# Layer 2 of a four-layer kernel: when VectorE adds an expert's output, and when two router and step-size pieces are issued

## The chip, the core and the metric

The kernel runs on one core of one Trainium2 chip. The metric is the device time of one execution in microseconds (us). The engines are TensorE (PE in the rows; PEld is its weight load), VectorE (DVE), ScalarE (ACT), GpSimd (POOL) and SyncE (SP). Each works through its own instructions in order and waits for the others at semaphores.

## The reference, cut to layer 2

Four layers, each `x = x + s * silu(f)` on 4 sequences of 512 tokens with 128 features, where `s` is a sequence mixer of the normed input and `f` a mixture of experts of the same input. The change is in layer 2: a selective scan, and 8 experts of which two count for a token.

```
dbc = einsum('ble,fe->blf', x_main, W_x)
dt_raw, Bm, Cm = dbc[..., :64], dbc[..., 64:80], dbc[..., 80:]
dt = softplus(einsum('blr,er->ble', dt_raw, W_dt) + b_dt)      # 256 step sizes a token
def step(h, inp):                                              # 16 states a feature
    h = exp(dt_t[..., None] * A) * h + dt_t[..., None] * B_t[:, None, :] * x_t[..., None]
    y = einsum('ben,bn->be', h, C_t)
...
logits = silu(xt @ rw1 + rb1) @ rw2 + rb2
w = softmax(where(mask_of_top_2, logits, -inf), axis=1)        # the shares
h = silu(einsum('nd,edh->enh', xt, we1) + be1)                 # 8 experts, 512 hidden
eo = einsum('enh,ehd->end', h, we2) + be2
y = xt + einsum('ne,end->nd', w, eo)
```

## The kernel before, in words

The four sequences are the batches b = 0 to 3 (`B`), a sequence is 4 tiles of 128 tokens (`T`), and layer 2 goes through 16 state steps a batch (`NS`), 64 in all: step k is step n = k % 16 of batch k // 16. The order on every engine is written out by hand in one loop over k for each; nothing schedules it.

In step k VectorE does, in this order: scan(k), the recurrence over all 512 tokens for both halves of the 256 features (one 128x1024 instruction, L2430 in the rows, with both its operands in SBUF); outs(k-1), two products with C (L2438, one operand in PSUM); inputs(k+2), the product of dt\*x with B (L2423, one operand in PSUM). After them, in even steps, comes add_expert: four additions of 128x128 (L2454), one for each tile of tokens, each of which adds one expert's output, weighed by its share, to `ACC2`. Steps 2, 4, 6, 7, 10, 11 and 13 hold more: normalisation, the second half of the last batch's output (L2483 first), the choice of experts, `split`, `share` (L2387 first; it needs the exponentials that ScalarE makes in share_exp) and dt_sums (L2408, L2410, then L2415 in dt_x). Step 12 holds `correction` (L2401) between the scan and outs.

GpSimd adds every product of outs to `YY` (L1985, two instructions a step, all operands in SBUF). H has four buffers.

TensorE in its step k: chunk(2k), the second product of an expert, c_row(k), which spreads C for outs(k) into a PSUM bank and waits for outs(k-1) to have read it, chunk(2k+1), b_row(k+3), the same for inputs(k+3), then one of the jobs that share PSUM bank 0 ("spare" jobs, table `front_order`), two hidden products of an expert, and then any second spare job of the step. In step 9 the spare jobs are the two products for the step sizes of the next batch, ("dt", 0) ahead of the hidden products and ("dt", 1) behind them. A spare job waits until its forerunner's bank has been read.

ScalarE makes the decays (L2270, two steps' worth in each even step, `wide` in the rows), the silus of the hidden products (L2258, four in each odd step), and for the next batch dt_parts (L2217, L2218), dt_exp (L2222), share_exp (L2226) and others.

Of the kernel before, what the change touches and what calls it, by code (L numbers as in the profile page):

```python
# [27 lines left out]
T = S // P  # L28
# [5 lines left out]
def build(nc, I, out):  # L34
    ctx = ExitStack()
    with ctx:
# [378 lines left out]
        def lsem(name):  # L415
            h = scope[0].enter_context(nc.semaphore(name))
            lsems.append(h)
            return h
# [1449 lines left out]
        def layer2(fcT, pjT, feats, wide, XM, mv3, rstd3):  # L1868
# [10 lines left out]
            hp, hs, op_, ad = (lsem(f"f2_{k}") for k in ("hidden", "silus", "chunks", "added"))  # L1879
# [9 lines left out]
            def use(*key):  # L1889
                uses[key] = len(uses)  # L1890
            front_order = {4: (("xnt",),), 5: (("r1",),), 6: (("logits",),), 7: (("c", 0), ("c", 1)), 8: (("dbc",),),
                           9: (("dt", 0), ("dt", 1)), 14: (("wT",),)}
            for key in (("xnt",), ("c", 0), ("c", 1), ("r1",), ("dbc",), ("dt", 0), ("dt", 1), ("logits",), ("wT",)):
                use(key[0], 0, *key[1:])
            first_bank = {("r1",): 5, ("c", 0): 6, ("c", 1): 7, ("dt", 0): 6, ("dt", 1): 7}
# [6 lines left out]
            for k in range(NK):  # L1902
                b, n = divmod(k, NS)
# [16 lines left out]
            def read(*key):  # L1920
                return uses[key] + 1

            with ExitStack() as c:
# [26 lines left out]
                with nc.Block() as block:  # L1950
# [216 lines left out]
                    def _(act):  # L2167
# [124 lines left out]
                        for k in range(NK):  # L2292
                            b, n = divmod(k, NS)
                            more = b + 1 < B
                            if n % 2 == 0 and k + 2 < NK:
                                decays(k + 2)
                                decays(k + 3)
                            if n == 7 and more:
                                x_silu(b + 1, 0)
                            if n == 9 and more:  # L2300
                                dt_parts(b + 1, 0)
                            if n == 13:
                                z_silu(b, 0)
                            if n == 1 and b:
                                gate(b - 1)
                            if n % 2 and k + 1 < NK:
                                for i in range(4):
                                    hidden(2 * k + 2 + i)
                            if n == 3 and more:
                                apply_in(b + 1)  # L2310
                            if n == 5 and b:
                                apply_out(b - 1)
                            if n == 4 and more:
                                turn_in(b + 1)
                            if n == 5 and more:
                                router(b + 1)
                            if n == 7 and more:
                                x_silu(b + 1, 1)
                            if n == 8 and more:
                                dbc(b + 1)  # L2320
                                d_term(b + 1)
                            if n == 9 and more:
                                dt_parts(b + 1, 1)
                            if n == 10 and more:
                                dt_exp(b + 1)
                                share_exp(b + 1)
                            if n == 12 and more:
                                dt_log(b + 1)
                            if n == 13:
                                z_silu(b, 1)  # L2330
                            if n == 14 and more:
                                store_wT(b + 1)
                            if not more and n in (3, 6, 9):
                                early_apply(n // 3 - 1)
                            if not more and n in (4, 7, 14):
                                early_turn((4, 7, 14).index(n))
# [15 lines left out]
                    def _(v):  # L2352
# [90 lines left out]
                            nc.vector.tensor_tensor(ACC[:, :, :].rearrange(flat), o, XN4[:, b, :, :].rearrange(flat),  # L2443
                                                    ALU.add).then_inc(m0, 1)

                        def add_expert(j):
                            b, e = divmod(j, NE)
                            v.wait_ge(op_, 4 * j + 4)
                            if e:
                                v.wait_ge(ad, j)  # L2450
                            else:
                                v.wait_ge(m0, read("bias", b))
                            for t in range(T):
                                last = nc.vector.scalar_tensor_tensor(ACC[:, t, :], PS[:, 6 + j % 2, t * P:(t + 1) * P],  # L2454
                                                                      WG2[:, b % 2, t, e:e + 1], ACC[:, t, :], ALU.mult, ALU.add)
                            last.then_inc(ad, 1)

                        def gated(b):
                            v.wait_ge(m0, read("z", b, 1))
# [44 lines left out]
                        for k in range(NK):  # L2504
                            b, n = divmod(k, NS)
                            more = b + 1 < B
                            scan(k)
                            if k == 0:
                                share(0)
                            if n == 12 and more:  # L2510
                                correction(b + 1)
                            if n == 1 and b:
                                gated(b - 1)
                            if n == 2:
                                biases(b)
                            if n == 4 and b:
                                take_out(b - 1)
                            if n == 7 and more:
                                take_logits(b + 1)
                            if k:  # L2520
                                outs(k - 1)
                            if k + 2 < NK:
                                inputs(k + 2)
                            if n % 2 == 0 and k:
                                add_expert(k // 2 - 1)
                            if n == 2 and more:
                                stats_in(b + 1)
                            if n == 4 and b:
                                out_stats(b - 1)
                            if n == 6 and b:  # L2530
                                finish(b - 1)
                            if n == 7 and more:
                                choose(b + 1)
                            if n == 10 and more:
                                split(b + 1)
                            if n == 11 and more:
                                share(b + 1)
                            if n == 13 and more:
                                dt_sums(b + 1)
                                dt_x(b + 1)  # L2540
                            if not more and n in (2, 5, 8):
                                early_stats((2, 5, 8).index(n))
# [12 lines left out]
                        for t in range(T):  # L2555
# [3 lines left out]
                            last = nc.vector.tensor_tensor(X4[:, B - 1, t, :], x, rest[:, t, :], ALU.add)  # L2559
# [710 lines left out]
```

## Time and profile before

| | us |
|---|---|
| median of 3 runs (lowest to highest) | 1391.28 (1389.5 to 1394.29) |
| the profiled execution: time | 1392.78 |
| the profiled execution: span from first to last instruction | 1391.0 |
| mean granted TensorE clock | 0.922 of full |
| layer 2's state steps | about 758 to 1178 in the span |

The profile is one execution. Its time is 1.5 us above the median, and 1.8 us lie outside its span. Busy shares are given for each engine; a wait is idle time of an engine just before an instruction, put down to the engine that ended it.

### The profile page before, as it was taken

The numbers are of one execution on the slowest core, as the hardware profiler recorded it, in microseconds if no ns is written. First come the engines' busy times: TensorE is split into PE (matmuls) and PEld (weight loads), VectorE is DVE, ScalarE is ACT, GpSimd is POOL, SyncE is SP. The second block draws the span as 40 slices with busy tenths as digits, with TensorE's granted clock in tenths as the row PEclk, the third lists the DMA queues.
The fourth block names the chain that finished last, engine by engine and source line by source line (L and its number), as shares of the span: only waits on it lengthen the run. The fifth ranks groups of instructions, "written<-read, shape, count | busy, mean of one in ns | idle before, by whom it ended". The sixth has DMA issues, their size and how long they took to land. (4 is left out here: it accounts for less than half of the span.)

```text
span 1391.0 us, 21029 instructions
## 1 busy us (share of the span) xinstructions
PE 1151.0 (83%) x7010; PEld 811.3 (58%) x7010; DVE 999.5 (72%) x2280; ACT 763.7 (55%) x1586; POOL 614.8 (44%) x607
## 2 busy tenths in 40 slices
PE   3999999999898879367766888888888977889995
PEld 1455665665465568156653655655645655668885
DVE  2466767678787727277765989989998999535555
ACT  1456556555544527144446867667768675345552
POOL 4243445444336834554100533733643565216672
PEclk9999999999999989589987999999899889799997
DMA  7400000000000023550000000000000000101113
GB/s 176 121 1 1 1 1 1 1 1 1 1 5 22 28 63 116 154 163 16 1 13 0 1 1 1 1 1 1 1 1 1 1 1 0 31 10 40 43 44 107
DMA packets 54443, 40.71 MB, mean 29 GB/s; under 512 B 13185, under 2 KB 46687, under 8 KB 54337
## 3 DMA queue, kind: packets, MB, share of 16 engines
q1 hardware_dynamic: 40994, 27.58, 6.8%
q0 software_dynamic: 4544, 9.32, 2.4%
q10 hardware_dynamic: 8800, 2.48, 0.9%
q8 instruction: 58, 0.95, 0.3%
q14 instruction: 47, 0.39, 0.1%
HBM read 26.32 MB, written 13.04 MB: 28 GB/s over the span
## 5 line engine op out<-in xcount | busy, mean ns | idle before, releaser
L780 POOL TENSOR_TENSOR PR<-PR,R 128x512 f32<-128x512 f32 (+3 forms) x128 | 160.3, 1264 | 233.1 <-DVE R L1275 232.5
L1985 POOL TENSOR_TENSOR YY<-YY,H 128x512 f32<-128x512 f32 x120 | 164.1, 1390 | 182.0 <-DVE H L2438 182.0
L410 PE MATMUL banks<-XT,we 128*128 128x128 f32 (+1 forms) x568 | 175.8, 442 | 14.0 <-ACT HH L2258 13.7
L1074 ACT ACTIVATE PR<-banks,NM 128x257 f32<-128x257 f32 (+3 forms) x256 | 132.2, 526 | 94.7 <-DVE NM L1247 93.0
L410 PEld LDWEIGHTS banks<-we,HH 128*128 128x128 f32 x1024 | 144.9, 205 | 35.7 <-issue 31.2
L2430 DVE TENSOR_TENSOR_SCAN H<-wide,H 128x1024 f32<-128x1024 f32 x64 | 164.1, 2564 | 0.2
L410 PE MATMUL banks<-we,HH 128*128 128x128 f32 x1024 | 145.1, 288 | 0.0
L410 PEld LDWEIGHTS banks<-XT,we 128*128 128x128 f32 x568 | 89.5, 201 | 65.5 <-issue 41.2
L2258 ACT ACTIVATE HH<-banks,be1f 128x512 f32<-128x512 f32 x128 | 83.4, 685 | 73.7 <-PE banks L410 72.8
L410 PE MATMUL banks<-BCR,SEL 96*128 96x512 f32 x128 | 67.1, 526 | 63.8 <-DVE H L2438 55.4
L410 PEld LDWEIGHTS banks<-PTS,V 128*64 128x64 f32 x1152 | 65.7, 138 | 83.4 <-issue 48.5
L410 PE MATMUL banks<-PTS,V 128*64 128x128 f32 (+1 forms) x1152 | 93.1, 296 | 24.1 <-issue 11.0
L1247 DVE TENSOR_REDUCE NM<-banks 128x2 f32<-128x514 f32 (+3 forms) x128 | 102.7, 823 | 3.3
L1256 DVE COPY PTS<-banks 128x384 f32<-128x384 f32 (+1 forms) x96 | 57.5, 599 | 60.7 <-PE banks L936 59.8
L410 PE MATMUL banks<-KT,QT 64*128 64x384 f32 (+3 forms) x512 | 96.2, 474 | 1.5 <-issue 0.8
L936 PE MATMUL banks<-ident,PR 128*128 128x128 f32 x640 | 92.5, 285 | 2.1 <-POOL PR L780 1.8
L936 PEld LDWEIGHTS banks<-ident,PR 128*128 128x128 f32 x640 | 73.4, 145 | 31.6 <-issue 31.6
L2438 DVE TENSOR_TENSOR H<-H,banks 128x512 f32<-128x512 f32 x128 | 80.8, 671 | 7.5 <-PE banks L410 7.5
L2270 ACT ACTIVATE wide<-feats,Aneg 128x512 f32<-128x512 f32 (+1 forms) x128 | 81.9, 710 | 0.4
L2423 DVE TENSOR_TENSOR H<-DTX,banks 128x1024 f32<-128x1024 f32 x64 | 77.5, 1212 | 1.1 <-PE banks L410 0.9
L410 PEld LDWEIGHTS banks<-BCR,SEL 96*128 96x128 f32 x128 | 26.3, 206 | 72.0 <-DVE H L2438 61.9
L2747 POOL DMA_INDIRECT XS<-xrows,GIX x39 | 38.3, 982 | 53.5 <-DVE GIX L3157 37.3
(568 smaller groups left out, 2445.9 us busy)
## 6 DMA issues: line engine op xcount, KB each, us to landing
xsort<-zrow SPq DMA_DIRECT2D x1, 3072.0 KB, 13.6
XS<-xsort SPq DMA_DIRECT2D x12, 256.0 KB, 2.9
ysort<-PTS SPq DMA_DIRECT2D x12, 256.0 KB, 2.2
pj_stage<-in_L_ffn_w_proj SPq DMA_DIRECT2D x1, 2048.0 KB, 11.9
we<-in_L_ffn_we SPq DMA_DIRECT2D x1, 2048.0 KB, 15.3
we<-yrows SPq DMA_DIRECT2D x8, 256.0 KB, 5.4
xrows<-XN SPq DMA_DIRECT2D x4, 256.0 KB, 3.4
out<-XN SPq DMA_DIRECT2D x4, 256.0 KB, 2.3
```

The source lines that it names most:

```text
L410: return nc.tensor.matmul(o, l, r, start=start, stop=stop)
L780: last = nc.gpsimd.tensor_tensor(p, p, R[:, T * q + t, :].unsqueeze(2).to_broadcast([P, 2, w]), ALU.mult)
L936: last = nc.tensor.transpose(PS[:, 4 + s, k * P:(k + 1) * P], PR0[:, q % 2, s, a:a + P], ident[:, :])
L1074: nc.scalar.activation(PR0[:, q % 2, s, OFF[t]:OFF[t] + w], ps2(n)[:, s, SLOT[t]:SLOT[t] + w], ACT.Exp, bias=NM[:, m, s:s + 1], accum_out= ...
L1247: last = nc.vector.tensor_reduce(NM[:, T * q + t, :], ps2(n)[:, :, SLOT[t]:SLOT[t] + (t + 1) * P + more], AX.X, ALU.max, negate=True)
L1256: nc.vector.tensor_copy(PTS[:, m % 2, 1, 0:w], PS[:, 5, 0:w]).then_inc(ptB, 1)
L1985: nc.gpsimd.tensor_tensor(YY[:, m, :], YY[:, m, :] if n else XD[m], H[:, k % 4, m, :], ALU.add).then_inc(ya, 1)
L2258: nc.scalar.activation(HH[:, i, :], PS[:, 3 + g % 3, :], ACT.Silu, bias=be1f[:, j % NE, i:i + 1]).then_inc(hs, 1)
L2270: nc.scalar.activation(DA[:, k % 4, m, m:], DT[:, b % 2, m, m:], ACT.Exp, scale=Aneg[:, m, n:n + 1]).then_inc(ex, 1)
L2423: nc.vector.tensor_tensor(H[:, k % 4, :, :], DTX[:, b % 2, :, :], PS[:, 1, :].unsqueeze(1).to_broadcast([P, 2, S]), ALU.mult).then_inc(bm, 1)
L2430: nc.vector.tensor_tensor_scan(h, DA[:, k % 4, :, :].rearrange("p m s -> p (m s)"), h, 0.0, ALU.mult, ALU.add).then_inc(scn, 1)
L2438: nc.vector.tensor_tensor(h, h, PS[:, 2, :], ALU.mult).then_inc(hc, 1)
```

## The change

Three things move; nothing is removed or added to the computation. In step 0 VectorE still adds the last batch's eighth expert whole. For the other experts it adds tiles 0 and 1 in an even step and tiles 2 and 3 in the odd step behind it, and tells TensorE that the bank is free only after the second half. `share` moves from step 11 to step 12. The product ("dt", 1) moves from the end of TensorE's step 9 to the place of step 10's first spare job, and ScalarE's dt_parts for it from step 9 to step 10, ahead of dt_exp.

```diff
--- before.py
+++ after.py
@@ -1889,7 +1889,7 @@
             def use(*key):
                 uses[key] = len(uses)
             front_order = {4: (("xnt",),), 5: (("r1",),), 6: (("logits",),), 7: (("c", 0), ("c", 1)), 8: (("dbc",),),
-                           9: (("dt", 0), ("dt", 1)), 14: (("wT",),)}
+                           9: (("dt", 0),), 10: (("dt", 1),), 14: (("wT",),)}
             for key in (("xnt",), ("c", 0), ("c", 1), ("r1",), ("dbc",), ("dt", 0), ("dt", 1), ("logits",), ("wT",)):
                 use(key[0], 0, *key[1:])
             first_bank = {("r1",): 5, ("c", 0): 6, ("c", 1): 7, ("dt", 0): 6, ("dt", 1): 7}
@@ -2319,9 +2319,8 @@
                             if n == 8 and more:
                                 dbc(b + 1)
                                 d_term(b + 1)
-                            if n == 9 and more:
+                            if n == 10 and more:
                                 dt_parts(b + 1, 1)
-                            if n == 10 and more:
                                 dt_exp(b + 1)
                                 share_exp(b + 1)
                             if n == 12 and more:
@@ -2443,17 +2442,18 @@
                             nc.vector.tensor_tensor(ACC[:, :, :].rearrange(flat), o, XN4[:, b, :, :].rearrange(flat),
                                                     ALU.add).then_inc(m0, 1)
 
-                        def add_expert(j):
+                        def add_expert(j, tiles=range(T)):
                             b, e = divmod(j, NE)
                             v.wait_ge(op_, 4 * j + 4)
                             if e:
                                 v.wait_ge(ad, j)
                             else:
                                 v.wait_ge(m0, read("bias", b))
-                            for t in range(T):
+                            for t in tiles:
                                 last = nc.vector.scalar_tensor_tensor(ACC[:, t, :], PS[:, 6 + j % 2, t * P:(t + 1) * P],
                                                                       WG2[:, b % 2, t, e:e + 1], ACC[:, t, :], ALU.mult, ALU.add)
-                            last.then_inc(ad, 1)
+                            if tiles[-1] == T - 1:
+                                last.then_inc(ad, 1)
 
                         def gated(b):
                             v.wait_ge(m0, read("z", b, 1))
@@ -2521,8 +2521,10 @@
                                 outs(k - 1)
                             if k + 2 < NK:
                                 inputs(k + 2)
-                            if n % 2 == 0 and k:
+                            if n == 0 and k:
                                 add_expert(k // 2 - 1)
+                            elif n > 1:
+                                add_expert(k // 2 - 1, (0, 1) if n % 2 == 0 else (2, 3))
                             if n == 2 and more:
                                 stats_in(b + 1)
                             if n == 4 and b:
@@ -2533,7 +2535,7 @@
                                 choose(b + 1)
                             if n == 10 and more:
                                 split(b + 1)
-                            if n == 11 and more:
+                            if n == 12 and more:
                                 share(b + 1)
                             if n == 13 and more:
                                 dt_sums(b + 1)
```

VectorE, batch 0's steps 11 and 12 before: `wide` holds the decays, `PR` and `OH` lead to the shares (`WG`), `EW` is the exponential of dt. Line numbers of the kernel before.

```order
L2430 SCALAR_TENSOR_TENSOR H<-wide,H 128x1024
L2438 TENSOR_TENSOR H<-H,banks 128x512 x2
L2423 TENSOR_TENSOR H<-DTX,banks 128x1024
L2387 TENSOR_TENSOR PR<-PR,OH 128x4x8
L2388 TENSOR_REDUCE rt<-PR 128x4
L2389 RECIPROCAL rt<-rt 128x4
L2390 TENSOR_TENSOR WG_9025<-PR,rt 128x32
L2430 SCALAR_TENSOR_TENSOR H<-wide,H 128x1024
```

The same steps in the changed kernel, where lines from here on have numbers lower by one: first step 11, then step 12 up to the scan of step 13.

```order
L2429 SCALAR_TENSOR_TENSOR H<-wide,H 128x1024
L2437 TENSOR_TENSOR H<-H,banks 128x512 x2
L2422 TENSOR_TENSOR H<-DTX,banks 128x1024
L2453 SCALAR_TENSOR_TENSOR ACC_9023<-banks,WG_9025,ACC_9023 128x128 x2
L2429 SCALAR_TENSOR_TENSOR H<-wide,H 128x1024
```

```order
L2429 SCALAR_TENSOR_TENSOR H<-wide,H 128x1024
L2400 TENSOR_SCALAR DTX<-EW 128x1024
L2401 TENSOR_TENSOR DTX<-EW,DTX 128x1024
L2437 TENSOR_TENSOR H<-H,banks 128x512 x2
L2422 TENSOR_TENSOR H<-DTX,banks 128x1024
L2453 SCALAR_TENSOR_TENSOR ACC_9023<-banks,WG_9025,ACC_9023 128x128 x2
L2386 TENSOR_TENSOR PR<-PR,OH 128x4x8
L2387 TENSOR_REDUCE rt<-PR 128x4
L2388 RECIPROCAL rt<-rt 128x4
L2389 TENSOR_TENSOR WG_9025<-PR,rt 128x32
```

Step 11 has two additions and no share rows; step 12 has two additions, and the four share rows stand behind them.

ScalarE, steps 9 to 10 of batches 0 to 2, as a difference: `feats` and `EW` are written by dt_parts, `wide` by the decays.

```order
+L2270 ACT_TABLE_LOAD
+L2270 ACTIVATE wide<-feats,Aneg 128x512
+L2270 ACTIVATE wide<-feats,Aneg 128x511
+L2270 ACTIVATE wide<-feats,Aneg 128x512
+L2270 ACTIVATE wide<-feats,Aneg 128x511
 L2217 ACTIVATE feats<-banks,bdt 128x512
 L2218 ACTIVATE EW<-banks,bdt 128x512
-L2270 ACT_TABLE_LOAD
-L2270 ACTIVATE wide<-feats,Aneg 128x512
-L2270 ACTIVATE wide<-feats,Aneg 128x511
-L2270 ACTIVATE wide<-feats,Aneg 128x512
-L2270 ACTIVATE wide<-feats,Aneg 128x511
```

The four decays come ahead of the second dt_parts instead of behind it; dt_exp and share_exp follow both.

TensorE, from the product ("dt", 0) of its step 9 on: `XNT,WdtT` are the dt products, `XT,we` hidden products, `we,HH` chunks, and `BCR,SEL` c_row, then b_row.

```order
 L410 MATMUL banks<-XNT,WdtT 128x512
 L410 MATMUL banks<-XT_9022,we_7451 128x512 x2
+L410 MATMUL banks<-we_7452,HH 128x128 x4
+L410 MATMUL banks<-BCR,SEL 128x512
+L410 MATMUL banks<-we_7452,HH 128x128 x4
+L410 MATMUL banks<-BCR,SEL 128x512
 L410 MATMUL banks<-XNT,WdtT 128x512
-L410 MATMUL banks<-we_7452,HH 128x128 x4
-L410 MATMUL banks<-BCR,SEL 128x512
-L410 MATMUL banks<-we_7452,HH 128x128 x4
-L410 MATMUL banks<-BCR,SEL 128x512
 L410 MATMUL banks<-XT_9022,we_7451 128x512 x2
```

Both chunks, c_row(10) and b_row(13) now come ahead of ("dt", 1).

## Rows read from the trace of the kernel before

**Rows 1.** The page, part 1: busy time, share of the span, instructions.

```profile
PE 1151.0 (83%) x7010; PEld 811.3 (58%) x7010; DVE 999.5 (72%) x2280; ACT 763.7 (55%) x1586; POOL 614.8 (44%) x607
```

**Rows 2.** Busy us by engine in layer 2; then TensorE clock and DMA.

```profile
740.00:1180.00 440.00, 359.41 (x1659) 244.17 (x1658) 410.99 (x599) 311.69 (x435) 206.04 (x164) 0.91 0.00 1
```

**Rows 3.** Group of the scans there: busy us, mean ns, idle before.

```profile
L2430 DVE TENSOR_TENSOR_SCAN H<-wide,H 128x1024 f32<-128x1024 f32 x64 | 164.1, 2564 | 0.2
```

**Rows 4.** Waits of VectorE there: total us, times, longest us.

```profile
DVE H L2438 <- PE banks L410: 7.5, 6, 3.2
DVE PR L2387 <- ACT PR L2226: 7.1, 3, 2.7
```

**Rows 5.** Timeline of VectorE, batches 0 and 1: start us, duration us.

```profile
857.40 1.25 DVE L2438 TENSOR_TENSOR H<-H,banks 128x512 f32<-128x512 f32 x2
...
859.71 3.15 DVE L2430 TENSOR_TENSOR_SCAN H<-wide,H 128x1024 f32<-128x1024 f32 x1
...
865.09 1.11 DVE L2454 SCALAR_TENSOR_TENSOR ACC<-banks,WG,ACC 128x128 f32<-128x128 f32 x4
866.12 2.27 DVE L2430 TENSOR_TENSOR_SCAN H<-wide,H 128x1024 f32<-128x1024 f32 x1
...
884.47 2.90 DVE L2430 TENSOR_TENSOR_SCAN H<-wide,H 128x1024 f32<-128x1024 f32 x1
```

**Rows 6.** Timeline of GpSimd in the same stretch.

```profile
858.20 2.50 POOL L1985 TENSOR_TENSOR YY<-YY,H 128x512 f32<-128x512 f32 x2 [3.03 <-DVE H L2438]
863.58 2.52 POOL L1985 TENSOR_TENSOR YY<-YY,H 128x512 f32<-128x512 f32 x2 [2.87 <-DVE H L2438]
...
883.95 4.48 POOL L1985 TENSOR_TENSOR YY<-YY,H 128x512 f32<-128x512 f32 x2
```

**Rows 7.** Timeline of VectorE, batch 0, steps 11 to 13; [idle before <-releaser].

```profile
827.34 1.29 DVE L2438 TENSOR_TENSOR H<-H,banks 128x512 f32<-128x512 f32 x2 [2.38 <-PE banks L410]
828.54 1.22 DVE L2423 TENSOR_TENSOR H<-DTX,banks 128x1024 f32<-128x1024 f32 x1
832.45 0.19 DVE L2387 TENSOR_TENSOR PR<-PR,OH 128x32 f32<-128x32 f32 x1 [2.69 <-ACT PR L2226]
...
833.22 2.28 DVE L2430 TENSOR_TENSOR_SCAN H<-wide,H 128x1024 f32<-128x1024 f32 x1
...
840.63 2.28 DVE L2430 TENSOR_TENSOR_SCAN H<-wide,H 128x1024 f32<-128x1024 f32 x1
...
845.14 2.08 DVE L2408 TENSOR_TENSOR feats<-feats,DTX 128x1024 f32<-128x1024 f32 x1
...
849.65 2.28 DVE L2430 TENSOR_TENSOR_SCAN H<-wide,H 128x1024 f32<-128x1024 f32 x1
```

**Rows 8.** Timeline of TensorE, its loop steps 9 and 10, batches 0 and 2.

```profile
822.54 2.08 PE L410 MATMUL banks<-XT,we 128*128 128x512 f32 x2 [2.50 <-ACT HH L2258]
824.41 1.77 PE L410 MATMUL banks<-XNT,WdtT 96*128 96x512 f32 x2
826.01 1.06 PE L410 MATMUL banks<-we,HH 128*128 128x128 f32 x8
826.82 0.48 PE L410 MATMUL banks<-BCR,SEL 96*128 96x512 f32 x1
...
1043.30 1.02 PE L410 MATMUL banks<-XNT,WdtT 96*128 96x512 f32 x2
```

**Rows 9.** Timeline of ScalarE, batch 0, the same place.

```profile
826.21 0.69 ACT L2217 ACTIVATE feats<-banks,bdt 128x512 f32<-128x512 f32 x1 [0.87 <-PE banks L410]
...
828.79 2.56 ACT L2270 ACTIVATE wide<-feats,Aneg 128x512 f32<-128x512 f32 x4
831.26 1.04 ACT L2222 ACTIVATE EW<-EW 128x1024 f32<-128x1024 f32 x1
```

**Rows 10.** Timeline of VectorE, outs(10) of batches 1 and 2.

```profile
938.75 1.29 DVE L2438 TENSOR_TENSOR H<-H,banks 128x512 f32<-128x512 f32 x2 [3.17 <-PE banks L410]
...
1045.48 1.28 DVE L2438 TENSOR_TENSOR H<-H,banks 128x512 f32<-128x512 f32 x2 [0.72 <-PE banks L410]
```

## The prediction

> **What bounds the kernel now.** The page shows TensorE busy 83% of the span and VectorE 72% [rows 1], but the change lies in one stretch, so I read the busy time of layer 2's stretch alone. There VectorE works 411.0 of 440 us, TensorE 359.4, ScalarE 311.7, GpSimd 206.0 [rows 2]. The state steps are VectorE's: scan, outs, inputs and additions follow each other without a gap almost everywhere, and the next layer starts only when layer 2's last output is done. So an idle or stretched microsecond of VectorE here is a microsecond of the kernel. Two things are to be seen in it. The list of its waits gives 7.5 us before outs (L2438, on TensorE) and 7.1 us before share (L2387, on ScalarE) [rows 4]; I then went to the timeline at those places. And the scan, always the same instruction, has a mean of 2564 ns over 64 [rows 3], while a single one takes 2.27 or 3.15 us [rows 5].
>
> **Why scans differ.** GpSimd starts its two additions to YY 0.8 us after outs starts (857.40, 858.20) and needs 2.50 us, to 860.70; the scan behind it starts at 859.71 and takes 3.15 us. A batch step later the four expert additions stand between (865.09, next scan 866.12, so 1.03 us for four), GpSimd's pair is over at 866.10, and the scan takes 2.27 [rows 5, 6]. The excess of 0.88 us is about the overlap of 0.99. The reverse is there too: at 883.95 a GpSimd pair takes 4.48 us around a scan that starts at 884.47 and takes 2.90 itself [rows 5, 6]. I read this as one of the two waiting for the other whole, for instructions with all operands in SBUF. L2408, with both operands in SBUF, shows the same: 2.08 us behind inputs [rows 7]; its neighbours take about 1.2. Outs, inputs and the expert additions read one operand from PSUM and keep their times.
>
> The Trainium skill, "SBUF — State Buffer", section "SBUF: two separate sides", says that a GpSimd instruction and a VectorE instruction with two SBUF inputs lock each other out, the first to start holding the shared ports to its end. The trace agrees: 0.88 us of delay for 0.99 of overlap. For a scan that comes late in GpSimd's instruction, which no row shows behind two additions, that rule would make term 1 the 5.4 us below; the rows alone leave it between a loss of 6.6 and a gain of 13.7 (the bounds below, at 23 places).
>
> **Term 1, the spread additions.** No addition goes away. Two take 1.03/2 = 0.52 us. So a scan that had nothing ahead of it gets 0.52 us of cover and keeps 0.88 - 0.52 = 0.36 of its delay; one that had four additions ahead goes from none to 0.36. This is an estimate, as no scan of the trace has two additions ahead of it; its bounds are 0 (any cover is enough) and 0.88 (any overlap costs as much as full). I take 0.36 since the one other partial overlap (2.90, an excess of 0.63, with GpSimd's first instruction in its way until 883.95 + 1.25 = 885.20, 0.73 after the scan's start) [rows 5, 6] fits a wait for the rest; it also speaks against both bounds. Where other work covers the scan anyway (normalisation, choice, split, share) nothing changes.
> For batches 0 to 2, with n the step of the scan: saved are 4 and 6 (late GpSimd pair, 0.5 each), 10 and the next batch's 0 (0.52 each) and L2408 in step 13 (0.5), 2.5 us; lost are 9, 12 and 15, 0.36 each, 1.1. That is 1.5 a batch. In batches 1 and 2 the output of the last batch (L2483 and on) in step 6 comes too early for GpSimd or ScalarE when its two additions leave, which gives back 0.5 each. Batch 3 has no next batch to prepare: saved 4, 6, 8, 10, 12 and 14 (3.1), lost 11 and 13 (0.7) and the output (0.5), 1.9. The end (steps 14 and 15) I count as nothing. Sum: 3 x 1.5 - 1.0 + 1.9 = 5.4 us.
>
> **Term 2, share in step 12.** Share waits 2.69 us in batch 0 for share_exp, from 829.76 to 832.45 [rows 7]; three such waits are 7.1 us [rows 4]. One step later VectorE comes for it after a scan, correction, outs and inputs, some 7 us on. ScalarE's pieces are the same in another order: its silus end at 826.21 - 0.87 = 825.34; from 826.21 to 831.26 it needs 5.05 us for dt_parts, a table load and decays [rows 9]; so dt_exp starts at about 830.4 and ends at 831.4. Its next user, `correction`, is due at about 831.9 (below). All 7.1 us go, with 0.5 us of margin behind them, which is what is late next. If the cover failed, `correction` would wait, by no more than the old share wait. TensorE needs the shares only at its step 14.
>
> **Term 3, ("dt", 1) behind c_row(10).** In batch 0 TensorE waits 2.50 us for a silu that stands behind the first dt_parts, then does hidden(23), ("dt", 1) from 824.41 to 826.01, chunk(20) from 826.01 to 826.82, and c_row(10); outs(10) starts 0.52 behind c_row, at 827.34, having waited 2.38 [rows 7, 8]. The 2.50 stay, as the silu stands where it stood. Without ("dt", 1), 1.60 us go, but its duration is 1.77 here and 1.02 in batch 2 [rows 8]: TensorE runs at its lower clock level, 1.2 GHz, behind its idle time. Then chunk(20) runs slow in its place and takes up to 0.8 more, which leaves a gain of 0.8 (1.6 at most). VectorE itself arrives 0.15 earlier by term 1. So outs(10) starts at 826.5 and waits about 1.7. In batch 1 (3.17 now) [rows 10] I take 2.1 left, and 0.6 more before inputs(13), since a slow chunk(21) makes b_row(13) late; in batch 2 (0.72) none. The waits of L2438 on TensorE other than these and 0.6 at the end come to 0.6, of which 0.2 stay. Kept: 1.7 + 2.1 + 0.6 + 0.2 = 4.6 of 7.5 - 0.6 + 7.1 = 14.0 for terms 2 and 3, which save 9.4 us.
>
> Behind outs(10) VectorE in batch 0 then needs 1.20 + 1.13 for outs and inputs, 0.52 for the half, 0.36 + 2.20 for the scan: `correction` at 826.5 + 5.4 = 831.9.
>
> **What the half bank costs TensorE.** The bank is free one half later, in an odd step. chunk(4j) waits for it; ahead of that chunk TensorE has b_row, which waits for the same inputs, and two hidden products, 2.08 us at the slow clock [rows 8] and about 1.0 at the fast one. The half ends 0.6 us behind inputs. So it costs nothing; were that cover gone, at most 0.6 us for each of 7 experts a batch, 16.8 in all, on TensorE first.
>
> **Sum.** 5.4 + 9.4 = 14.8; I round to 14.5 for the waits between the estimates. The profiled execution took 1392.8, so 1378.3; it stands 1.5 above the median 1391.3, so 1376.8, said as 1377.
>
> **The rivals.**
> *Waits come back elsewhere.* TensorE and ScalarE are both near full at steps 8 to 13, and VectorE now arrives 3 us earlier at step 12. If it waits there for dt_exp, dt_log or a bank for all it won, only term 1 is left: 1391.3 - 5.4 = 1386. For it: ScalarE has margins of 0.5 us only. Against: from step 12's scan on VectorE has no wait in batch 0 [rows 7], though it loses 3 us of lead here.
> *Partial overlap costs full.* 23 places (six in each of batches 0 to 2, five in batch 3) are half covered. If each pays 0.88 instead of 0.36, 12.0 us go, and 2.5 are left: 1389. Against it: the excess of 0.63.
> *Slower: GpSimd wins every contest.* If GpSimd's second addition is always served first and the scan waits a whole one, 2.50/2 = 1.25 us, each half-covered scan costs 0.89 more than I take: 23 x 0.89 = 20.5 against 14.5, so 1391.3 + 6 = 1397. It becomes slower than before from 0.63 us more at each place. Against it: a full overlap costs only 0.88 now.
> *The change does nothing*, because what it moves was hidden: excluded for the waits, as nothing runs on VectorE during them.
>
> **How the numbers follow.** Forecast 0.74 (own range 1372 to 1382); waits come back 0.12; partial costs full 0.08; slower 0.06. The lower end is all 14.0 us of waits gone and term 1 whole: 19.4, so 1372. The upper end is between the forecast and the rivals; 1386 takes the first one in. 0.3% is 4.2 us, about what a measurement of this kernel can tell from no change. The first rival lies beyond it by 1.2, so a quarter of its chance is counted within: faster 0.74 + 0.09 + 0.02 = 0.85, same 0.10, slower 0.05.
>
> **What would show it.** Right: no wait at share; outs(10) of batch 0 waiting about 1.7 us, of batch 2 near none; scans behind two additions at 2.6 to 2.7 us, none at 3.15 except in step 2 and perhaps at the end; the mean of the scans near 2485 ns (5.1 us over 64 scans less). Wrong: scans of 3.1 us in steps 9, 12 and 15, or new waits at `correction`, at L2410 in step 13 (dt_log late), or before outs in steps 11 and 12.

## The result and the profile after

The changed kernel takes 1381.99 us in the median of 6 runs (1376.58 to 1384.44), the kernel before 1390.2 (1388.27 to 1394.29) beside it. The ratio is 0.9927 with a 95% interval from 0.9906 to 0.9948: about 10 us faster, between 7 and 13; the two medians alone are 8.2 us apart. Run once more beside later experiments it gave 0.9908 (0.9889 to 0.9927). The range 1372 to 1386 holds the time. The 14.5 us forecast, a ratio of 0.9896, are more than the result and just outside the first interval, though inside the second.

The changed kernel's stretch of layer 2, columns as in [rows 2]:

```profile
740.00:1171.00 431.00, 358.22 (x1672) 246.54 (x1672) 408.10 (x602) 312.42 (x436) 208.46 (x164) 0.92 0.00 1
```

The engines are busy for nearly as long as before (VectorE 408.1 us for 411.0); it is the stretch that is shorter. How much is best read from one line per kernel, the list of the scan's 64 instructions: shortest, median and longest in ns, then the start of the first and of the last in us. First the kernel before, then the changed one:

```profile
L2430 DVE TENSOR_TENSOR_SCAN H<-wide,H x64: 2256/2288/3231, 758.3 to 1170.6; 128x1024 f32<-128x1024 f32 x64
```

```profile
L2429 DVE TENSOR_TENSOR_SCAN H<-wide,H x64: 2254/2393/3172, 758.5 to 1158.2; 128x1024 f32<-128x1024 f32 x64
```

From the first scan to the last it was 1170.6 - 758.3 = 412.3 us and is 1158.2 - 758.5 = 399.7. So the state steps gave 12.6 us in this pair of executions; the spans (1391.0, 1379.9) differ by 11.1, so 1.5 were lost outside the steps, 1.3 of them behind the last scan. Below I call this length "the state steps" and read it for each kernel from the same kind of line. It tells more than the whole time does, since the part behind the last scan varies from execution to execution: 220 and 222 us in this pair, 230 to 238 in the experiments, where the kernel before took some 1405 us. So ratios are compared with ratios and state steps with state steps.

VectorE's waits in the stretch, to be laid beside [rows 4]:

```profile
DVE H L2437 <- PE banks L410: 6.0, 5, 2.2
...
DVE ACC L2442 <- PE banks L410: 2.2, 4, 0.7
...
DVE H L2422 <- PE banks L410: 1.3, 3, 0.9
```

The wait at share is not in the list any more: 7.1 us are gone. L2437, which was L2438, still waits 6.0 of 7.5. Two small waits for TensorE that were there before have grown: at L2442 (L2443 before) from 1.4 to 2.2 us, at L2422 (L2423 before) from 0.9 to 1.3. The scans' group, beside [rows 3]:

```profile
L2429 DVE TENSOR_TENSOR_SCAN H<-wide,H 128x1024 f32<-128x1024 f32 x64 | 158.2, 2472 | 0.2
```

Their sum fell from 164.1 to 158.2 us. A place behind two additions, VectorE first, then GpSimd in the same moment:

```profile
849.32 1.21 DVE L2422 TENSOR_TENSOR H<-DTX,banks 128x1024 f32<-128x1024 f32 x1
850.45 0.60 DVE L2453 SCALAR_TENSOR_TENSOR ACC<-banks,WG,ACC 128x128 f32<-128x128 f32 x2
850.97 2.63 DVE L2429 TENSOR_TENSOR_SCAN H<-wide,H 128x1024 f32<-128x1024 f32 x1
```

```profile
848.95 2.51 POOL L1985 TENSOR_TENSOR YY<-YY,H 128x512 f32<-128x512 f32 x2 [6.52 <-DVE H L2437]
```

GpSimd's pair ends at 851.46, the scan comes at 850.97 and takes 2.63: 0.36 more than 2.27, and not 0.88 or 1.25. Steps 11 and 12 of batch 0, beside [rows 7]: VectorE, TensorE, ScalarE.

```profile
825.69 1.28 DVE L2437 TENSOR_TENSOR H<-H,banks 128x512 f32<-128x512 f32 x2 [1.70 <-PE banks L410]
827.08 1.22 DVE L2422 TENSOR_TENSOR H<-DTX,banks 128x1024 f32<-128x1024 f32 x1
...
828.74 2.44 DVE L2429 TENSOR_TENSOR_SCAN H<-wide,H 128x1024 f32<-128x1024 f32 x1
831.10 0.66 DVE L2400 TENSOR_SCALAR DTX<-EW 128x1024 f32<-128x1024 f32 x1
...
835.79 0.54 DVE L2386 TENSOR_TENSOR PR<-PR,OH 128x32 f32<-128x32 f32 x1
```

```profile
822.03 1.49 PE L410 MATMUL banks<-XT,we 128*128 128x512 f32 x2 [2.50 <-ACT HH L2258]
823.31 1.92 PE L410 MATMUL banks<-we,HH 128*128 128x128 f32 x8
824.88 0.78 PE L410 MATMUL banks<-BCR,SEL 96*128 96x512 f32 x1
```

```profile
828.02 0.66 ACT L2217 ACTIVATE feats<-banks,bdt 128x512 f32<-128x512 f32 x1
...
829.29 1.06 ACT L2222 ACTIVATE EW<-EW 128x1024 f32<-128x1024 f32 x1
```

outs(10) waits 1.70 us, where 1.7 was foretold; the share rows start at 835.79 without a wait, though their first takes 0.54 us where it took 0.19; TensorE still waits its 2.50 for the silu; dt_exp starts at 829.29 and correction at 831.10 finds it done by 0.75 us.

### The profile page after: what moved, and what is told of

Read it like the earlier page. It is cut to its first block and busy times, and to the rows that moved or that the text cites. A ratio compares the mean times of both kernels' runs of the same rounds, so it can differ in the third digit from the quotient of the medians.

```text
span 1379.9 us, 21057 instructions
## 1 busy us (share of the span) xinstructions
PE 1145.9 (83%) x7010; PEld 811.0 (59%) x7010; DVE 993.6 (72%) x2280; ACT 763.3 (55%) x1586; POOL 617.3 (45%) x607
## 5 line engine op out<-in xcount | busy, mean ns | idle before, releaser
L410 PE MATMUL banks<-XT,we 128*128 128x128 f32 (+1 forms) x568 | 173.0, 437 | 11.3 <-ACT HH L2258 11.0
L2429 DVE TENSOR_TENSOR_SCAN H<-wide,H 128x1024 f32<-128x1024 f32 x64 | 158.2, 2472 | 0.2
L2437 DVE TENSOR_TENSOR H<-H,banks 128x512 f32<-128x512 f32 x128 | 80.8, 671 | 6.1 <-PE banks L410 6.0
L2422 DVE TENSOR_TENSOR H<-DTX,banks 128x1024 f32<-128x1024 f32 x64 | 77.6, 1213 | 1.7 <-PE banks L410 1.3
```

The costliest lines, as they stand in the source:

```text
L410: return nc.tensor.matmul(o, l, r, start=start, stop=stop)
L2422: nc.vector.tensor_tensor(H[:, k % 4, :, :], DTX[:, b % 2, :, :], PS[:, 1, :].unsqueeze(1).to_broadcast([P, 2, S]), ALU.mult).then_inc(bm, 1)
L2429: nc.vector.tensor_tensor_scan(h, DA[:, k % 4, :, :].rearrange("p m s -> p (m s)"), h, 0.0, ALU.mult, ALU.add).then_inc(scn, 1)
L2437: nc.vector.tensor_tensor(h, h, PS[:, 2, :], ALU.mult).then_inc(hc, 1)
```

## The experiments

Each run has a profile and, where a ratio is given, runs beside the kernel before. The state steps are one execution each.

**The three parts one by one.** The code is the diff above with the other parts undone.

Share alone:

```diff
-                            if n == 11 and more:
+                            if n == 12 and more:
                                 share(b + 1)
```

> The kernel before with share alone moved to step 12. My theory (VectorE's idle time in the state steps is kernel time): the 7.1 us of waits for share_exp go and nothing takes their place, so about 1390.2 - 7 = 1383; one scan a batch (step 12) is bare now and pays up to 0.9 us, so 1383 to 1386. Rival (the waits come back at the next place that needs ScalarE, correction or dt_sums): 1388 to 1390, with new waits at L2401 or L2410 of 1.5 us or more each.

Measured: ratio 0.9959 (0.9943 to 0.9976), so 3 to 8 us of 1405.65 where 4 to 7 were expected, and 1163.3 - 760.4 = 402.9 us of state steps, 9.4 less than before:

```profile
L2430 DVE TENSOR_TENSOR_SCAN H<-wide,H x64: 2257/2291/3235, 760.4 to 1163.3; 128x1024 f32<-128x1024 f32 x64
```

Its waits, in the list of waits of VectorE:

```profile
DVE H L2438 <- PE banks L410: 3.8, 3, 2.4
...
DVE H L2430 <- ACT wide L2270: 1.4, 3, 0.5
```

Nothing waits at correction or dt_sums; the rival falls. A small new wait stands at the scan of step 12 for the decays (1.4 us in three). L2438 waits only 3.8 us here, and that is not share's doing: TensorE's clock stayed up in two of its batches, as shown below.

("dt", 1) alone:

```diff
-                           9: (("dt", 0), ("dt", 1)), 14: (("wT",),)}
+                           9: (("dt", 0),), 10: (("dt", 1),), 14: (("wT",),)}
...
-                            if n == 9 and more:
+                            if n == 10 and more:
                                 dt_parts(b + 1, 1)
-                            if n == 10 and more:
                                 dt_exp(b + 1)
```

> The kernel before with (dt, 1) and its dt_parts alone moved to step 10. My theory: outs(10) starts 0.8 to 1.6 us earlier in each batch, but share still waits in step 11 for share_exp, which ends only 0.5 to 0.9 us earlier, so the gain is what share_exp gains: 1.5 to 2.5 us in all, 1388 to 1389. Rival (each move has its whole gain by itself): 2.6 us and more, below 1387.6.

Measured: ratio 1.0001 (0.9985 to 1.0018), state steps 412.3 us (760.3 to 1172.6), nothing gained.

```profile
DVE PR L2386 <- ACT PR L2226: 9.5, 3, 3.4
DVE H L2437 <- PE banks L410: 4.1, 7, 1.5
```

The wait before outs fell to 4.1 us, but the wait at share rose from 7.1 to 9.5: what outs(10) won, share gave back in the same step. The 1.5 to 2.5 us that I expected do not show; the ratio's interval leaves room for 2 us either way. The rival, 2.6 us and more, falls.

The halves alone:

```diff
-                            if n % 2 == 0 and k:
+                            if n == 0 and k:
                                 add_expert(k // 2 - 1)
+                            elif n > 1:
+                                add_expert(k // 2 - 1, (0, 1) if n % 2 == 0 else (2, 3))
```

> The kernel before with the additions alone split over even and odd steps. By the lock theory scans behind two additions take 2.63 us, and the sum of the scans falls by 5 us; share and outs(10) still wait, and in steps 8 to 11 what VectorE wins turns into waiting there. So a gain of 2 to 4 us, 1386 to 1388. Rival (the split gives its whole 5 us by itself): 1385. Rival (the split is worth nothing, all comes from the two moves): 1390.

Measured: ratio 0.9946 (0.9924 to 0.9968), so 4 to 11 us of 1405.65; state steps 404.1 us:

```profile
L2430 DVE TENSOR_TENSOR_SCAN H<-wide,H x64: 2256/2392/3172, 753.7 to 1157.8; 128x1024 f32<-128x1024 f32 x64
```

```profile
DVE H L2438 <- PE banks L410: 9.9, 5, 3.5
DVE PR L2387 <- ACT PR L2226: 4.6, 3, 1.8
```

That is 8.2 us less than before, more than the 2 to 4 expected and than the first rival's 5; it is one execution, and the ratio's 4 to 11 us still allow a gain at the top of my estimate. By the brackets of its timeline, VectorE's time outside waits fell by 5.9 us and its waits by 2.3. The share wait is 4.6 for 7.1: two additions of step 11 now fill 0.52 us of it in each of three batches, and they were a cost elsewhere before. I had counted waits as swallowing what VectorE wins; they also take up work for nothing.

Share and ("dt", 1) without the halves, against the changed kernel:

```diff
-                            if n == 0 and k:
+                            if n % 2 == 0 and k:
                                 add_expert(k // 2 - 1)
-                            elif n > 1:
-                                add_expert(k // 2 - 1, (0, 1) if n % 2 == 0 else (2, 3))
```

> The changed kernel with an expert's four additions whole in the even step, so share and (dt, 1) alone moved. My theory: the waits are worth 8 us, so 1382 to 1384, 1 to 3 us above the changed kernel; scans of 3.15 us stand in steps 0, 2, 6, 10 and 12. Rival (the two moves without the spread additions gain nothing, as scans take it back): 1388 and more. Rival (the spread additions are worth nothing): the time of the changed kernel, 1380 to 1382.

Measured: ratio 0.9940 (0.9919 to 0.9962), state steps 405.2 us:

```profile
L2429 DVE TENSOR_TENSOR_SCAN H<-wide,H x64: 2256/2291/3245, 756.5 to 1161.7; 128x1024 f32<-128x1024 f32 x64
```

So the halves are worth 5.5 us of state steps on top of the two moves (405.2 against 399.7), and the moves 7.1 without the halves. That 5.5 is so near term 1's 5.4 is chance: VectorE's time outside waits falls by 7.8 (397.4 to 389.6), because without the halves the scan of step 12 stands bare once share has left (3.15, 2.68 and 3.17 us in the three batches, 2.28 before), and its waits rise by 2.3 (7.8 to 10.1). The first rival falls, and so does the second in the state steps; the ratios (0.9940 with, 0.9927 and 0.9908 for the changed kernel) overlap.

**Is ("dt", 1) worth anything in the changed kernel?** Its place and dt_parts back in step 9, the rest as changed, beside the changed kernel itself:

> The changed kernel once more, as the measure for the three runs beside it. 0.992 to 0.994 of the kernel before; state steps 399 to 402 us from the first scan to the last.

> The changed kernel with (dt, 1) and its dt_parts back in step 9. Theory A (moving them pays only where TensorE's clock has fallen, 0.9 us a batch, and else 0.05): the state steps take 399 to 402 us, as long as the changed kernel's, at most 2 us more. Theory B (term 3 of the prediction, 0.8 to 1.6 us in every batch): 402 to 404 us, 2.4 us and more above it.

Measured: after_again 0.9908 (0.9889 to 0.9927), share_halves 0.9918 (0.9903 to 0.9934). State steps 399.1 and 396.7:

```profile
L2429 DVE TENSOR_TENSOR_SCAN H<-wide,H x64: 2256/2398/3171, 759.0 to 1158.1; 128x1024 f32<-128x1024 f32 x64
```

```profile
L2430 DVE TENSOR_TENSOR_SCAN H<-wide,H x64: 2255/2390/3167, 755.0 to 1151.7; 128x1024 f32<-128x1024 f32 x64
```

The intervals overlap, so the move is worth nothing that this can tell; the single execution without it is even the shorter. Theory B falls by the state steps of this pair; the ratios alone would not exclude its 2.4 us. The waits say where the time went: before the three outs(10) VectorE waits 3.6 us with the move and 6.9 without it, so the move does shorten the wait it was made for; but all its other waits come to 5.1 with the move and 0.5 without. What makes those larger is not shown. Why the wait before outs(10) varies is seen in share_only, whose batches 0 and 1 have the same order and the same gap on TensorE but not the same granted clock (column PEclk). Two windows of 5 us, each from about 0.6 us before that gap ends:

```profile
core 0: us, PE busy (x) PEld busy (x) DVE busy (x) ACT busy (x) POOL busy (x), PEclk, DMA share, GB/s
824.00:829.00 5.00, 4.40 (x13) 2.43 (x14) 2.97 (x2) 3.11 (x6) 0.00 (x0) 0.66 0.00 0
931.50:936.50 5.00, 4.47 (x23) 3.22 (x24) 4.27 (x5) 4.75 (x7) 0.48 (x1) 1.00 0.02 5
```

and TensorE's ("dt", 1) in them, batch 0 and batch 1:

```profile
826.47 1.77 PE L410 MATMUL banks<-XNT,WdtT 96*128 96x512 f32 x2
```

```profile
933.00 1.02 PE L410 MATMUL banks<-XNT,WdtT 96*128 96x512 f32 x2
```

Just ahead of each TensorE has waited 2.50 us, until 824.60 and 932.03. In batch 0 the mean grant fell to 0.66 of the higher level, 2.4 GHz, ("dt", 1) took 1.77 us, and outs(10) waited 2.39; in batch 1 it stayed at 1.00, the product took 1.02, and outs(10) waited 0.70. The same move saves 0.9 us in the one case (1.47 left in dt_only, batch 0, where the mean grant is 0.66 too) and 0.05 in the other (0.66 and 0.65 left, at 1.00). So the clock behind the gap decides what the move is worth, and the gap alone does not decide the clock: it is 2.50 us in both.

**Take that idle time away.** The silu that TensorE waits for stands behind the first dt_parts on ScalarE, which itself waits for ("dt", 0) (2.54 us in batch 0 of the changed kernel), and behind a table load. There ScalarE does, before TensorE goes on at 822.03:

```profile
819.99 1.28 ACT L2258 ACT_TABLE_LOAD   x1
821.29 1.84 ACT L2258 ACTIVATE HH<-banks,be1f 128x512 f32<-128x512 f32 x3
```

With the silus ahead of dt_parts, table load and silus no longer wait for ("dt", 0):

```diff
-                            if n == 9 and more:
-                                dt_parts(b + 1, 0)
                             if n == 13:
                                 z_silu(b, 0)
...
                             if n % 2 and k + 1 < NK:
                                 for i in range(4):
                                     hidden(2 * k + 2 + i)
+                            if n == 9 and more:
+                                dt_parts(b + 1, 0)
```

> The changed kernel with the first dt_parts behind the four silus of ScalarE's step 9. Theory A (the wait of 2.5 us on TensorE for a silu behind dt_parts and a table load is the cause of what is left before outs(10)): that wait goes, VectorE's waits for TensorE in steps 9 to 11 fall from 5.6 us to 1.5 at most, and the state steps take 396 to 397 us. Theory B (ScalarE is full there, and the decays or dt_exp come late instead): waits of scan(12) or correction take its place, and the state steps take 399 us or more.

Measured: ratio 0.9843 (0.9827 to 0.9859), 22 us below the kernel before and 9 below the changed kernel beside it (1383.06 against 1391.98); state steps 393.3 us:

```profile
L2429 DVE TENSOR_TENSOR_SCAN H<-wide,H x64: 2256/2394/3176, 752.6 to 1145.9; 128x1024 f32<-128x1024 f32 x64
```

TensorE at the same place as 822.03 above, here in batch 1: ("dt", 0), both pairs of hidden products in one row without a wait, chunk(20), c_row(10).

```profile
915.82 1.02 PE L410 MATMUL banks<-XNT,WdtT 96*128 96x512 f32 x2
916.67 1.88 PE L410 MATMUL banks<-XT,we 128*128 128x512 f32 x4
918.39 1.05 PE L410 MATMUL banks<-we,HH 128*128 128x128 f32 x8
919.20 0.48 PE L410 MATMUL banks<-BCR,SEL 96*128 96x512 f32 x1
```

```profile
815.20:820.20 5.00, 5.00 (x27) 3.52 (x27) 4.97 (x5) 4.97 (x9) 1.34 (x2) 1.00 0.00 0
918.60:923.60 5.00, 5.00 (x28) 3.52 (x27) 4.97 (x5) 4.97 (x7) 1.33 (x2) 1.00 0.01 3
1022.10:1027.10 5.00, 5.00 (x28) 3.51 (x27) 4.97 (x5) 4.97 (x7) 1.33 (x2) 1.00 0.00 0
```

The clock stays at 1.00 in all three batches, and in VectorE's list of waits L2437 has 1.7 us left of 6.0. Theory A holds, and by more than it said: all waits fall from 8.7 us in after_again to 3.4, which is 5.3 of the 5.8 us of state steps. The gap and the slow clock behind it went together, so what each of them cost is not separated. The move of ("dt", 1) is what allows this order: in step 9 the product would wait for the first dt_parts with TensorE behind it. That was argued from the code and not run.

**Where cover counts.**

```diff
+                                pair = n // 2
+                                if pair in (4, 7) or pair == 2 and b == 0 or pair in (5, 6) and not more:
+                                    even, odd = (0, 1), (2, 3)
+                                elif pair == 3 and more:
+                                    even, odd = (0, 1, 2, 3), ()
+                                else:
+                                    even, odd = (), (0, 1, 2, 3)
```

> As late_parts, and the additions placed where no other work covers the next scan: whole in the odd steps 3, 5, 11 and 13, whole in step 6, two and two in 8 and 9, 14 and 15 (batch 0 also 4 and 5; batch 3 two and two from step 8 on). By the lock theory each of the scans of steps 4, 6 and 12 and L2408 loses 0.1 to 0.4 us: 1 to 1.3 us a batch, 3 to 4 us in all below late_parts. Rival (where the cover stands doesn't matter): the time of late_parts.

Measured: ratio 0.9874 (0.9853 to 0.9894), 1387.69 us beside 1383.06 for late_parts, where I expected 3 to 4 less; state steps 1154.6 - 757.4 = 397.2, 3.9 more. VectorE in step 3 and its next scan, and GpSimd:

```profile
877.54 1.12 DVE L2453 SCALAR_TENSOR_TENSOR ACC<-banks,WG,ACC 128x128 f32<-128x128 f32 x4
878.58 3.11 DVE L2429 TENSOR_TENSOR_SCAN H<-wide,H 128x1024 f32<-128x1024 f32 x1
```

```profile
877.03 2.51 POOL L1985 TENSOR_TENSOR YY<-YY,H 128x512 f32<-128x512 f32 x2
```

GpSimd's pair is late here, as normalisation's small steps stand ahead of it. Its first instruction ends at 877.03 + 1.25 = 878.28. With four additions ahead the scan comes at 878.58, when the second has begun, and pays 0.84; with two it comes inside the first, slips in between them, and takes 2.39. So more cover cost more, in six scans (3.10 or 3.11 us, 0.71 more each; one of batch 0, two each of batches 1 and 2, one of batch 3). My expectation took GpSimd's pair as one block; it is two instructions, and the order of arrival decides. That is half of the loss. The other half I had not counted: with whole additions in odd steps or step 6, the first SBUF instructions of the choice (L2380, step 7), `split` (L2393, step 10) and share (L2386, step 12) stand bare and take 0.83, 1.17 and 1.05 us for 0.32, 0.67 and 0.54, 4.6 us over three batches. The scans of step 12 and L2407 win 1.1 us each.

Three and one in place of two and two:

```diff
-(0, 1) if n % 2 == 0 else (2, 3)
+(0, 1, 2) if n % 2 == 0 else (3,)
```

> The changed kernel with three additions in the even and one in the odd step. Linear cover (what is left of GpSimd's pair is what a scan waits): scans behind three additions take about 2.38, those behind one 2.89, so the pair costs as much as with two and two; behind GpSimd's late pair (scans 4 and 6) 2.65 for 2.39. State steps 400 to 402 us. Rival (a scan that meets GpSimd at all pays in full): 3.15 behind one addition and 3.15 behind three.

Measured: ratio 0.9900 (0.9872 to 0.9928), state steps 401.8. A scan behind three additions and one behind one:

```profile
912.05 2.38 DVE L2429 TENSOR_TENSOR_SCAN H<-wide,H 128x1024 f32<-128x1024 f32 x1
...
917.63 2.90 DVE L2429 TENSOR_TENSOR_SCAN H<-wide,H 128x1024 f32<-128x1024 f32 x1
```

2.38 and 2.90: the delay falls by 0.26 us with each addition, as what is left of GpSimd's pair, 0.62 and 0.10 over 2.28 and in sum as much as twice 0.36. The rival falls. The state steps are within what I expected and some 2 us longer than the changed kernel's (399.7 and 399.1): the scans behind GpSimd's late pair take 2.65 for 2.39, as expected.

**Without the lock.** GpSimd's additions cut to 8 of 512 tokens in steps 1 to 15, in the kernel before and in the changed one; both leave out most of layer 2's sum over the states.

```diff
-YY[:, m, :], YY[:, m, :] if n else XD[m], H[:, k % 4, m, :]
+YY[:, m, q], YY[:, m, q] if n else XD[m], H[:, k % 4, m, q]      # q = 0:8, whole for n == 0
```

> The kernel before with GpSimd's additions to YY cut to 8 of 512 tokens (but for step 0), so that layer 2's output lacks most of them; waits and order are unchanged. Lock theory: the scans take 2.27 us wherever GpSimd was in their way, only those of step 2 stay at 3.15, the sum of the 64 falls from 164 to about 149, L2408 from 1.87 to 1.23 us a time; the waits for share_exp and for TensorE in steps 9 to 11 grow, as VectorE comes earlier. Rival (long scans come from TensorE's or ScalarE's traffic or from the scan's own inputs): the sum stays near 164.

> The same cut in the changed kernel. Without the lock only the moves of share and (dt, 1) tell the two apart: by the sum of term 1 and terms 2 and 3, the state steps of thin_after are shorter than those of thin_before by the waits alone, 7 to 9 us, where the whole change gave 12.6; scans at 2.27 us. Rival (the spread additions have a worth beside the lock): 12 us again.

Measured, one run each: 1383.4 and 1370.1 us beside 1404.95. The scans' group in both, then the scans' first and last starts:

```profile
L2431 DVE TENSOR_TENSOR_SCAN H<-wide,H 128x1024 f32<-128x1024 f32 x64 | 149.5, 2335 | 0.2
```

```profile
L2430 DVE TENSOR_TENSOR_SCAN H<-wide,H 128x1024 f32<-128x1024 f32 x64 | 149.4, 2334 | 0.2
```

```profile
L2431 DVE TENSOR_TENSOR_SCAN H<-wide,H x64: 2256/2282/3181, 752.5 to 1150.2; 128x1024 f32<-128x1024 f32 x64
```

```profile
L2430 DVE TENSOR_TENSOR_SCAN H<-wide,H x64: 2257/2281/3179, 752.3 to 1138.3; 128x1024 f32<-128x1024 f32 x64
```

The sum is 149.4 or 149.5 in both: the long scans of the kernel before were GpSimd's. The four that stay long, up to 3.18 us, are those of step 2, where GpSimd still adds all tokens. But the state steps are 397.7 and 386.0, still 11.7 apart, where I expected 7 to 9 from the waits alone and the rival said 12. The arithmetic that failed is the addition: in thin_before VectorE comes earlier and waits 4.4 us more in all (21.7 for 17.3, the brackets of its timeline from the first to the last scan summed), so waits and lock are not two separate stores. In thin_after it waits 10.6, so 11.1 of the 11.7 us are waits. Outside the waits (376.0 and 375.4) the spread additions have no worth left, but what they do to the waits (2.3 us in halves_only) is in the 11.1 and is not separated here, so the rival is not excluded. And in thin_after `correction` waits 1.7 us in all for dt_exp: with VectorE this much faster, waits do come back where the first rival of the prediction looked for them.

## Why the prediction was right, and where its size was off

**What bounds.** Right: idle or stretched time of VectorE in the state steps was kernel time, 12.6 us there and 11.1 in the span.

**Term 1.** Right in mechanism; right in size partly by luck. I forecast 5.4; VectorE's time outside waits fell from 395.0 to 389.6 us (the state steps less the brackets of the timeline). A scan at half cover takes the 2.63 us of the estimate. But my list of places was off both ways, by about 2.6 us each way.

Lost and not foretold: batch 0 has no last batch's output in steps 4 and 6, so its scans 5 and 7 lost cover (0.51 and 0.36 us); scan 5 meets GpSimd's long row:

```profile
785.69 2.83 DVE L2429 TENSOR_TENSOR_SCAN H<-wide,H 128x1024 f32<-128x1024 f32 x1
```

```profile
779.40 6.96 POOL L1985 TENSOR_TENSOR YY<-YY,H 128x512 f32<-128x512 f32 x4
```

`split`'s copy, which reads and writes SBUF only, takes 0.66 us in three batches where it took 0.42, and 0.42 again in thin_after (columns as in the scan's line above); and share's first row, behind two additions, takes 0.54 for 0.19 in three batches (835.79 above), and 0.18 in thin_after.

```profile
L2393 DVE CAST BCR<-XNT x4: 420/656/658, 741.0 to 1031.2; 32x512 fp32r<-32x512 f32 x4
```

Won and not foretold: a small instruction of the choice (L2380) that now comes behind the additions takes 0.31 us for 0.84 in three batches; the scans of step 12, for which I had counted 0.36 each, lose 0.16, 0.01 and 0.09, with inputs late before them; and the output of batch 3 costs 0.26 for 0.5. In batches 1 and 2 the output's first step (0.69 and 0.72 before, 1.23 now) loses the 0.5 foretold:

```profile
L2483 DVE TENSOR_TENSOR XN<-XN,gamma x3: 799/1231/1234, 899.3 to 1111.9; 128x512 f32<-128x512 f32 x3
```

**Term 2.** Right: 7.1 us of waits gone, nothing in their place in the changed kernel, with a margin of 0.75 at correction where I said 0.5; in after_again correction did wait, 0.2 us in two batches.

**Term 3.** This is the term that was mis-sized. I put what is kept of the waits before outs and inputs at 4.6 of 6.9 us, and terms 2 and 3 at 9.4. All waits in the state steps fell from 17.3 to 10.1, by 7.2: 6.5 are left before outs and inputs, and the others rose from 3.3 to 3.6. In batch 0 the wait is as foretold (1.70), partly by luck: outs(10) starts at 825.69, where I had 826.5, and VectorE is ready for it at 823.99, where I had 824.8. In batch 2 I took 0.72 as given and foretold none; its TensorE clock fell this time (a mean grant of 0.73 in the window from 1032 to 1037), and outs(10) waited 2.2. I read the slow clock as a property of the batches, and it is one of the execution: ahead of outs(10) it fell in batches 0 and 1 of the kernel before, in all three of the changed one, and in batch 0 alone of share_only, dt_only and after_again. By dt_only and share_halves the move of ("dt", 1) is worth nothing that can be measured by itself.

**Half bank.** No wait of TensorE for it was found: in the state steps of the changed kernel its list of waits names outs, the silus and three others of 1.5 us or less, and not the additions.

**The rivals.** "Waits come back elsewhere" did not come true in the changed kernel; "partial overlap costs full" and "GpSimd wins every contest" fall by 2.63 us, though a place for the last exists: in placed_late the scan pays for GpSimd's second instruction when it comes after that has begun.

**The tail.** 1.3 us of the 12.6 were lost behind the last scan in this pair (220.4 before, 221.7 after), which the prediction put at nothing. Over all kernels here that part varies by more, and I have no cause for it.

## What to carry to other kernels

Where VectorE and GpSimd both work out of SBUF, look at what stands between their instructions: a piece with a PSUM operand that has to be done anyway shortens the wait there by its own length, up to what remains of the instruction it covers. Look also at when that instruction ends and at what loses its cover: placed_late lost time both ways. A wait of one engine on another is also a place for work. And when a product on TensorE is slow behind an idle gap, remove the gap before moving the product: here moving it gave nothing that could be measured by itself, and closing the gap gave 6 us of the state steps and 9 of the median.

## What the runs showed of the hardware that was not expected

GpSimd's additions and VectorE's instructions with all operands in SBUF exclude each other by whole instructions, and the delay is linear in the overlap: 0.88, 0.62, 0.36, 0.10 and 0 us behind none, one, two, three and four additions of 0.26. The first four belong to overlaps of 0.99, 0.75, 0.49 and 0.23 us, so each delay is the overlap less 0.11 to 0.13. The Trainium skill, "SBUF — State Buffer", section "SBUF: two separate sides", states that whichever of the two starts first holds the shared ports for its whole instruction and the other is blocked; these five points agree with it. The same idle gap of 2.50 us on TensorE was followed by a mean grant of 0.66 in one batch and 1.00 in another of one execution (share_only), and outs(10) behind it waited 2.39 or 0.70 us.
